# A graph layer's edge phase on TensorE as a loop, with its node phase and its loads reordered

## The chip, the core and the metric

The kernel runs on one core of a Trainium2 chip. A core has five engines that run their own instruction streams and meet only through semaphores: TensorE (PE, matrix products and transposes), VectorE (DVE), ScalarE (ACT), GpSimd (POOL) and SyncE (SP, which here only issues DMAs). The time is that of one execution on the device, in microseconds (us). The profile is of one execution of its own, whose time stands beside the others below.

## What is computed

The layer has 6250 nodes with 64 features and 200,000 directed edges, sorted by their destination. Each node is normed and goes through a small two-layer network. Each edge takes its two nodes' vectors, mixes them through three matrices and eight basis values, applies a second small network, and adds the outcome to its destination node.

```python
h = jnp.maximum(_layernorm(x, axis=-1), 0.0)
p1 = jnp.tanh(h @ pp_W1 + pp_b1) @ pp_W2 + pp_b2
inter = jnp.concatenate([p1[idx_i], p1[idx_j]], axis=-1)
inter = inter @ pi_W1 + pi_b1
inter = inter @ pi_W2 + pi_b2
inter = inter @ pi_W3
inter = inter.reshape(inter.shape[0], D, N_BASIS)
i1 = jnp.einsum('ecb,eb->ec', inter, basis)
i1 = jnp.tanh(i1 @ ii_W1 + ii_b1) @ ii_W2 + ii_b2
out = jax.ops.segment_sum(i1, idx_j, num_segments=p1.shape[0])
x = x + out
```

## The kernel before

**Node phase.** The matrices before the edge's basis values are linear, so the kernel folds them. A node's share as source (`u_tab`, 64 floats a row) and its share as destination (`v_tab`, three bf16 parts that sum to the float) are computed once for each node and stored to memory. For this PE transposes and multiplies the weights (L914, L918, L930; the products L925 to L928 make one constant that later becomes the bias `s_bias`), then takes the nodes in seven chunks: transposes (L873), first layer (L885), u rows (L891, copied by DVE at L610 and stored by SP at L298), and behind them v rows (stored at L306). The local places of each edge within its group, `loc_tab`, are stored too (L301).

**Edge phase.** The sorted edges are taken in 391 groups of 512 (`NG`), four tiles of 128. All engines run over the same steps. Step n does on PE, in this order: `sum_v(n)` (L982), which spreads the destination rows of a window of 42 nodes (`v_win`) over the edges by the one-hot `hot_t`; `place_rows(n)` (L987), which adds the gathered source rows `u_rows` and raises `s_ready`; `transpose_parts(n)` (L993) and `spread_basis(n-1)` (L1000) for the basis values; `z_group(n-2)` (L1008), 16 products whose outcome ACT puts through tanh (L517); the sum over destinations of group n-3 (L1050); and the transposes of group n-2 (L1015), which wait for that tanh. ACT also copies the sums to `st_sb` (L529, four times a group) and casts the basis (L539) and `t_sb` (L520). DVE multiplies by the basis (L693), makes the one-hots (L748, L794), splits the basis values of a whole piece into bf16 parts (L720 to L733), and adds the sums of a window to `acc_all` (L773), which it sets to zero at L756.

POOL issues four indirect gathers (L385) for each group into a ring of 16 slots (`UR`). It waits for `s_ready` of the group 16 before. SP fetches for each group the places (`loc_bc`, L327) and the window (`v_win`, L331), two rings of four slots, and every 15 groups (`PIECE`) a piece of `src`, `dst` and the basis values (L273, L274). If the graph isn't of the expected kind a slow path is taken; L1018 on PE is the jump past one of the two. PE's edge phase is written out: every step has its own instructions, and what it waits for are constants.

## Time and profile before

| | us |
|---|---|
| runs, median of three (lowest, highest) | 2676.39 (2671.01, 2684.13) |
| the profiled execution | 2664.88 |
| its span on the core | 2663.1 |
| L385 POOL, 1564 gathers, busy | 1515.0 |
| L693 DVE, 391 products, busy | 893.0 |
| L1008 PE, 6256 products, busy | 972.3 |
| L529 ACT, 1564 copies, busy | 734.3 |

A row of the timeline gives start, duration, engine, line and operation, and in brackets how long the engine sat idle before it and what ended that. "issue" is a wait that nothing in the profile shows; "remote" is a release from a queue that the profile can't name. PEld is the loading of weights into the array. SPq is the queue of an engine's own instructions, in which its DMAs are issued. A row of windows gives, for each stretch, its length, the busy time of each engine and its number of instructions, the granted TensorE clock as a share of 2.4 GHz, the busy share of 16 DMA engines and their rate. Between about 165 and 2566 us the groups run with gathers beside them; ahead of that stands the start, and behind it a few groups whose gathers are all done.

### The profile page before, as it was taken

Reading aid. Unit: us, or ns where it says so; the run is one execution under the profiler, and the core shown is the slowest. Engines: PE = TensorE matmul, PEld = TensorE weight load, DVE = VectorE, ACT = ScalarE, POOL = GpSimd, SP = SyncE. Lnnn points to the kernel's source line nnn. Section 1 sums busy time; section 2 is a strip of 40 time slices with the busy share of each in tenths; the row PEclk is TensorE's granted clock in tenths of the full one; section 3 lists DMA queues with packets and bytes.
Section 4 is the critical chain, followed back from the end, with each engine's and each line's share of the span. In section 5 each row is a group of like instructions: output and inputs, shape, how many; then the busy total and the mean of one; then the engine's idle time right before and its main releaser. Section 6 shows DMA issues by size and latency. Waiting matters only on the chain.

```text
span 2663.1 us, 55773 instructions
## 1 busy us (share of the span) xinstructions
PE 1994.9 (75%) x20333; PEld 1278.1 (48%) x20333; DVE 1261.5 (47%) x1823; ACT 1145.2 (43%) x2799; POOL 1521.3 (57%) x1581
## 2 busy tenths in 40 slices
PE   4147777878777777777877777778777778777788
PEld 3024454545454444444554454445444555444556
DVE  4224544545444444444454454454454444454455
ACT  4124444444444444444444444444444444444454
POOL 2755655656666555656565666566566565566530
PEclk9568888888988889888788888888888887888898
DMA  3212212222222221222221221222222122221111
GB/s 95 71 32 47 51 44 47 50 45 48 51 48 46 48 47 44 51 45 46 48 51 42 49 49 45 49 48 45 49 48 50 43 48 49 46 49 46 43 41 35
DMA packets 311481, 128.38 MB, mean 48 GB/s; under 512 B 233447, under 2 KB 283481, under 8 KB 311209
## 3 DMA queue, kind: packets, MB, share of 16 engines
q1 hardware_dynamic: 260033, 73.19, 13.6%
q0 software_dynamic: 50048, 51.35, 9.0%
q8 instruction: 165, 2.70, 0.4%
q14 instruction: 107, 0.88, 0.1%
q10 hardware_dynamic: 1128, 0.26, 0.1%
HBM read 118.67 MB, written 6.00 MB: 47 GB/s over the span
## 4 chain that ended last, share of the span: by engine, by line
PE 68%; issue 18%; another core or an unknown queue 7%; ACT 4%; DMA 1%; ACTq 0%; DVE 0%; SPq 0%; DVEq 0%
PE bank L1008 32%; PE bank L987 10%; PE bank L1050 8%; PE bank L1015 8%; PE spread_ps L1000 5%; PE bank L982 3%; ACT st_sb L529 3%; PE bank L993 1%; ACT tt_sb L517 1%; DMA v_tab<-acc_all 1%; DMA z_bias<-L_gnn_ii_b 0%; PE spread_ps L1083 0%; ACT t_sb L520 0%; ACT o_sb L438 0%
## 5 line engine op out<-in xcount | busy, mean ns | idle before, releaser
L385 POOL DMA_INDIRECT u_rows<-u_tab,src_e x1564 | 1515.0, 969 | 1044.0 <-PE bank L987 598.4
L693 DVE TENSOR_TENSOR o_sb<-st_sb,spread_ps 128x2048 f32<-128x2048 f32 x391 | 893.0, 2284 | 354.6 <-PE spread_ps L1000 182.2
L1008 PE MATMUL bank<-o_sb,g_sb 128*64 128x256 f32 x6256 | 972.3, 460 | 101.9 <-issue 92.7
L529 ACT ACTIVATE st_sb<-bank,s_bias 64x256 f32<-64x256 f32 x1564 | 734.3, 470 | 14.9
L1008 PEld LDWEIGHTS bank<-o_sb,g_sb 128*64 128x64 f32 x6256 | 529.2, 165 | 402.6 <-issue 284.0
L1015 PE MATMUL bank<-ident,tt_sb 128*128 128x128 f32 x782 | 183.6, 319 | 477.3 <-issue 356.1
L773 DVE TENSOR_TENSOR acc_all<-acc_all,bank 65x42 f32 x391 | 76.4, 195 | 977.4 <-remote 739.4
L517 ACT ACTIVATE tt_sb<-bank,z_bias 128x256 f32<-128x256 f32 x391 | 185.5, 474 | 724.3 <-remote 420.2
L520 ACT COPY t_sb<-bank 128x256 f32<-128x256 f32 x391 | 146.5, 375 | 515.3 <-PE bank L1015 406.4
L1015 PEld LDWEIGHTS bank<-ident,tt_sb 128*128 128x128 f32 x782 | 83.3, 149 | 521.8 <-issue 384.4
L987 PE MATMUL bank<-ident,u_rows 128*128 128x128 f32 x1564 | 320.8, 335 | 0.0
L1050 PEld LDWEIGHTS bank<-hot,t_sb 128*65 128x65 f32 x3128 | 224.7, 144 | 178.2 <-issue 177.4
L1050 PE MATMUL bank<-hot,t_sb 128*65 128x42 f32 x3128 | 272.4, 240 | 3.2 <-issue 2.7
L987 PEld LDWEIGHTS bank<-ident,u_rows 128*128 128x128 f32 x1564 | 236.4, 217 | 40.5 <-issue 9.7
L1000 PE MATMUL spread_ps<-bt_sb,spread 24*128 24x128 bf16 x6256 | 181.6, 241 | 14.2 <-issue 14.1
L539 ACT CAST bt_sb<-bank 128x128 bf16<-128x128 f32 x391 | 104.7, 268 | 198.4 <-remote 88.9
L982 PE MATMUL bank<-hot_t,v_win 126*64 126x128 bf16 x1564 | 125.3, 243 | 35.8 <-issue 35.7
L1000 PEld LDWEIGHTS spread_ps<-bt_sb,spread 24*128 24x128 bf16 x6256 | 103.6, 102 | 89.8 <-issue 89.7
L748 DVE TENSOR_SCALAR hot_t<-loc_bc,iota_p 126x512 bf16<-126x512 bf16 x391 | 142.3, 364 | 3.1 <-DMA loc_bc<-loc_tab 1.8
L794 DVE TENSOR_TENSOR hot<-loc_e,iota_f 128x168 f32<-128x168 f32 x391 | 126.2, 323 | 0.0
L982 PEld LDWEIGHTS bank<-hot_t,v_win 126*64 126x64 bf16 x1564 | 57.5, 112 | 109.8 <-issue 109.8
L993 PE MATMUL bank<-ident_b,b_parts 128*128 128x128 bf16 x391 | 94.9, 243 | 0.0
(110 smaller groups left out, 276.9 us busy)
## 6 DMA issues: line engine op xcount, KB each, us to landing
loc_bc<-loc_tab SPq DMA_DIRECT2D x391, 126.0 KB
u_rows<-u_tab,src_e POOLq DMA_INDIRECT x1564
v_win<-v_tab SPq DMA_DIRECT2D x391, 15.8 KB
basis<-edge_attr SPq DMA_DIRECT2D x26, 240.0 KB
v_tab<-acc_all SPq DMA_DIRECT2D x6, 375.0 KB
u_tab<-u_rows SPq DMA_DIRECT2D x6, 250.0 KB
out<-x_sb SPq DMA_DIRECT2D x2, 750.0 KB
x_sb<-x SPq DMA_DIRECT2D x3, 375.0 KB
```

The costliest lines, as they stand in the source:

```text
L385: pool.indirect_dma_start(out=u_rows[:, g % UR, j, :], out_offset=None, in_=u_tab[:, :], in_offset=bass.IndirectOffsetOnAxis(ap=src_e[:, g ...
L517: return nc.scalar.activation(tt_sb[:, r, :], z_ps, ACT.Tanh, bias=z_bias[:, 0:1])
L520: return nc.scalar.copy(t_sb[:, r, :, 0:D].rearrange("p (h q) c -> p q h c", h=2), t_ps.rearrange("p (q h c) -> p q h c", q=2, h=2))
L529: last = nc.scalar.activation(tiles[h * D:(h + 1) * D, j], s_ps[r][part].rearrange("p (q e) -> p q e", q=2), ACT.Identity, bias=s_bias[par ...
L693: return nc.vector.tensor_tensor(o_sb[:, r, :, :].rearrange("p c (j e) -> p j c e", j=TILES), st_sb[:, r, :].rearrange("p (j e) -> p j e", ...
L748: nc.vector.tensor_scalar(hot_t[:, g % 2, :], loc_bc[0:3 * W, g % VR, :], iota_p[0:3 * W, 0:1], None, ALU.is_equal).then_inc(hot_t_ready, 1)
L982: nc.tensor.matmul(s_ps[g % 2][TWICE[j], q * P:(q + 1) * P], v_win[:, g % VR, :], hot_t[:, g % 2, tile * P:(tile + 1) * P], start=(q == 0) ...
L987: last = nc.tensor.matmul(s_ps[r][:, q * P:(q + 1) * P], rows[:, 2 * q:2 * q + 2, :].rearrange("p j k -> p (j k)"), ident[:], start=alone ...
L1000: last = nc.tensor.matmul(spread_ps[:, j, c * P:(c + 1) * P], spread[q, 2 * c:2 * c + 2, :].rearrange("p b k -> p (b k)"), bt_sb[q, r, :], ...
L1008: last = nc.tensor.matmul(z_ps[h * D:(h + 1) * D, 0:2 * P], g_sb[:, c, :], o_sb[:, r, c, 2 * h * P:(2 * h + 2) * P], start=(c == 0), stop= ...
L1015: last = nc.tensor.transpose(t_ps[:, q * P:(q + 1) * P], tt_sb[:, r, q * P:(q + 1) * P], ident[:])
L1050: last = nc.tensor.matmul(seg_ps, t_sb[:, g % 2, j, :], hot[:, g % HR, j, :], start=(j == 0), stop=(j == TILES - 1))
```

## The change

Three things change together.

1. PE's steps 0 to 15 are written out, steps 16 to 383 are a loop of 23 passes over 16 steps, and steps 384 to 395 are written out again. In the loop, values that waits compare with, and the place in `b_parts`, are computed by register instructions. A piece now has 16 groups in place of 15, so that places in the rings are constants within the body.
2. In the node phase `wraw` and `p2` have a semaphore of their own, `w2_in`, and PE's first products wait for these three loads alone. The products of the weights stand in a row ahead of the first transposes. The constant's products and the copy to `s_bias` stand behind the u rows. ACT does the three weight copies ahead of its first root, and norms and tanhs in another order. The u rows are now staged in the basis buffer's far columns.
3. SP issues piece 1 behind the stores of u and v, in place of ahead of `loc_tab`'s store, and then waits for the u stores too. DVE sets the sums to zero behind the first group's splits and one-hots, and waits for this ahead of its first sum.

```diff
-    PIECE = 15
-    PIECES = FULL // PIECE
+    PIECE = 16
+    PIECES = -(-FULL // PIECE)
+    UN = UR
+    LOOP_END = NG // UN * UN
...
-        u_out = u_rows[0:NP].rearrange("p r j d -> p (r j) d")
+        u_out = basis[0:NP, 8 * PIECE * NBT:8 * PIECE * NBT + NPP * D].rearrange("p (i d) -> p i d", d=D)
...
-            load_piece(1)
             sp.wait_ge(loc_made, 1)
             sp.dma_start(loc_tab.rearrange("(b q) e -> q b e", b=RB),
...
+            load_piece(1)
             sp.wait_ge(base_read, 2)
...
             sp.wait_ge(loc_stored, 16)
+            sp.wait_ge(u_stored, 16 * NC)
...
             with dve.If(is_fast):
-                nc.vector.memset(acc, 0.0).then_inc(acc_zero, 1)
                 split_first(0)
...
                 pick_t(0)
-                dve.wait_ge(acc_zero, 1)
+                zero_sums()
                 for n in STEPS:
+                    if n == 4:
+                        dve.wait_ge(acc_zero, 1)
...
             pe.wait_ge(consts, 1)
-            pe.wait_ge(weights_in, 16 * N_WEIGHTS)
+            pe.wait_ge(w2_in, 48)
...
-            transposes(0)
             pe.wait_ge(wprep_act, 2)
             for half in TWICE:
-                const = bank[6][half, 0:1]
-                nc.tensor.matmul(const, a12[:, 0, :], b2col[:], start=True, stop=False)
...
             last.then_inc(wprep_pe, 1)
+            transposes(0)
             transposes(1)
...
+            pe.wait_ge(weights_in, 16 * N_WEIGHTS)
+            for half in TWICE:
+                const = bank[6][half, 0:1]
...
+            def step(n, u, first, last_pass):
+
+                def of(lag):
+                    return has_group(n, u, lag, first, last_pass)
+
+                def seen(lag, more=0):
+
+                    return n + (u - lag + 1 + more)
+
+                if of(0):
+                    pe.wait_ge(v_in[u % VR], n * (16 // VR) + 16 * (u // VR + 1))
+                    pe.wait_ge(hot_t_ready, seen(0))
...
             with pe.If(is_fast):
-                for n in STEPS:
...
+                for u in range(UN):
+                    step(0, u, True, False)
+                with pe.Fori(UN, LOOP_END, UN) as n:
+                    for u in range(UN):
+                        step(n, u, False, False)
+                for n in range(LOOP_END, NG + 5, UN):
+                    for u in range(UN):
+                        step(n, u, False, True)
```

PE's instructions at a step's boundary in the written-out edge phase, before:

```order
L1050 MATMUL bank<-hot,t_sb 65x42 x3
L1015 MATMUL bank<-ident,tt_sb 128x128 [waits tt_ready]
L1015 MATMUL bank<-ident,tt_sb 128x128
L982 MATMUL bank<-hot_t,v_win 64x128 [waits st_ready,hot_t_ready,v_in3]
L982 MATMUL bank<-hot_t,v_win 64x128 x3
L987 MATMUL bank<-ident,u_rows 128x128 [waits u_in3]
L987 MATMUL bank<-ident,u_rows 128x128
L993 MATMUL bank<-ident_b,b_parts 128x128
L1000 MATMUL spread_ps<-bt_sb,spread 128x128 [waits o_ready,bt_ready]
```

After, on PE where the loop begins (L1036 are the transposes, L1003 is `sum_v`, L1008 `place_rows`, L1021 `spread_basis`):

```order
L1036 MATMUL bank<-ident,tt_sb 128x128
L1085 UNCONDITIONAL_BRANCH
L1085 ISA
L1050 REGISTER_ALU [waits v_in0]
L1052 REGISTER_ALU [waits hot_t_ready]
L1003 MATMUL bank<-hot_t,v_win 64x128 [waits st_ready]
L1003 MATMUL bank<-hot_t,v_win 64x128 x3
L1054 REGISTER_ALU
L1008 MATMUL bank<-ident,u_rows 128x128 [waits u_in0]
L1008 MATMUL bank<-ident,u_rows 128x128
L1057 ISA
L1014 REGISTER_ALU [waits part3_]
```

The same operations stand in the same order; register instructions stand between them, and at the end of the body the loop's own pair, `L1085 REGISTER_ALU` and `L1085 COMPARE_AND_BRANCH`, follows the last transposes.

PE's start in the node phase, before, where L873 are the first transposes and L925 to L928 the constant's products:

```order
L914 MATMUL bank<-ident,wraw 64x64 [waits weights_in,consts]
L914 MATMUL bank<-ident,wraw 64x64 x2
L918 MATMUL bank<-p,wt 64x64 [waits wprep_act]
L918 MATMUL bank<-p,wt 64x64
L873 MATMUL spread_ps<-ident,o_sb 128x125 [waits normed_v]
L873 MATMUL spread_ps<-ident,o_sb 128x125 x3
L925 MATMUL bank<-b2col,a 64x1 [waits wprep_act]
L926 MATMUL bank<-b2col,a 64x1
L927 MATMUL bank<-pb1col,p 64x1
L928 MATMUL bank<-ones,b2row 64x1
L930 MATMUL bank<-a,wt 64x128
```

After (L925 is now the weights' transpose, L884 the nodes' transposes):

```order
L925 MATMUL bank<-ident,wraw 64x64 [waits w2_in,consts]
L925 MATMUL bank<-ident,wraw 64x64 x2
L929 MATMUL bank<-p,wt 64x64 [waits wprep_act]
L929 MATMUL bank<-p,wt 64x64
L934 MATMUL bank<-a,wt 64x128 [waits wprep_act]
L934 MATMUL bank<-a,wt 64x128
L884 MATMUL spread_ps<-ident,o_sb 128x125 [waits normed_v]
L884 MATMUL spread_ps<-ident,o_sb 128x125 x3
```

The first wait is for `w2_in` in place of `weights_in`, and the constant's products are gone from this place.

SP's queue from the u stores on, before:

```order
L298 DMA u_tab<-u_rows 125x512 [waits u_ready] x6
L298 DMA u_tab<-u_rows 125x128 [waits u_ready]
L273 DMA src_e<-src 128x15x4
L273 DMA dst_e<-dst 128x15x4
L274 DMA basis<-edge_attr 128x15x32
L301 DMA loc_tab<-loc_rows 98x4x512 [waits loc_made]
L306 DMA v_tab<-acc_all 125x1536 [waits v_ready] x6
L306 DMA v_tab<-acc_all 125x384 [waits v_ready]
L310 TENSOR_LOAD fast [waits flag_ready,base_read]
L310 ISA x2
L315 COMPARE_AND_BRANCH [waits v_stored3,v_stored2,loc_stored,v_stored1,v_stored0]
```

After, where the same pieces load at L275 and L276:

```order
L300 DMA u_tab<-basis 125x512 [waits u_ready] x6
L300 DMA u_tab<-basis 125x128 [waits u_ready]
L302 DMA loc_tab<-loc_rows 98x4x512 [waits loc_made]
L307 DMA v_tab<-acc_all 125x1536 [waits v_ready] x6
L307 DMA v_tab<-acc_all 125x384 [waits v_ready]
L275 DMA src_e<-src 128x16x4
L275 DMA dst_e<-dst 128x16x4
L276 DMA basis<-edge_attr 128x16x32
L312 TENSOR_LOAD fast [waits flag_ready,base_read]
L312 ISA x2
L318 COMPARE_AND_BRANCH [waits v_stored3,loc_stored,v_stored2,u_stored,v_stored1,v_stored0]
```

Piece 1 moved behind the seven stores of v, and stands next to piece 2, which follows the jump.

## Rows read from the trace of the kernel before

**Rows 1.** Windows by stage, the columns in the first row.

```profile
core 0: us, PE busy (x) PEld busy (x) DVE busy (x) ACT busy (x) POOL busy (x), PEclk, DMA share, GB/s
90.00:165.00 75.00, 12.83 (x76) 6.57 (x77) 6.29 (x11) 6.80 (x16) 49.95 (x53) 0.50 0.16 37
165.00:1000.00 835.00, 643.95 (x6588) 411.09 (x6588) 402.99 (x563) 367.36 (x904) 498.27 (x516) 0.86 0.24 47
1000.00:2560.00 1560.00, 1216.99 (x12337) 773.07 (x12336) 752.36 (x1047) 689.58 (x1693) 934.53 (x968) 0.86 0.23 47
2562.00:2640.00 78.00, 75.58 (x906) 49.28 (x902) 53.41 (x75) 49.55 (x120) 3.54 (x4) 1.00 0.11 26
```

**Rows 2.** Windows of L385 alone: us, POOL busy (x), PEclk, DMA share, GB/s.

```profile
200.00:2560.00 2360.00, 1411.96 (x1464) 0.86 0.23 47
```

**Rows 3.** Waits of POOL, 200 to 2560 us: total, times, longest.

```profile
POOL u_rows L385 <- PE bank L987: 580.2, 338, 4.8
```

**Rows 4.** Timeline, 1003 to 1018 us: start, duration, instruction [idle before <-releaser].

```profile
1007.28 1.07 POOL L385 DMA_INDIRECT u_rows<-u_tab,src_e  x1 [1.68 <-PE bank L987]
...
1007.33 1.95 PE L1008 MATMUL bank<-o_sb,g_sb 128*64 128x256 f32 x16
...
1010.82 0.47 ACT L517 ACTIVATE tt_sb<-bank,z_bias 128x256 f32<-128x256 f32 x1 [1.64 <-remote]
1011.16 0.94 POOL L385 DMA_INDIRECT u_rows<-u_tab,src_e  x1 [0.30 <-issue]
...
1011.35 0.44 PE L1015 MATMUL bank<-ident,tt_sb 128*128 128x128 f32 x2 [1.47 <-issue]
```

**Rows 5.** Timeline, ACT alone, 2595 to 2625 us.

```profile
2598.83 0.47 ACT L517 ACTIVATE tt_sb<-bank,z_bias 128x256 f32<-128x256 f32 x1
...
2602.98 0.47 ACT L517 ACTIVATE tt_sb<-bank,z_bias 128x256 f32<-128x256 f32 x1
...
2607.14 0.47 ACT L517 ACTIVATE tt_sb<-bank,z_bias 128x256 f32<-128x256 f32 x1
```

**Rows 6.** The page: DMA queue of the instructions.

```profile
q8 instruction: 165, 2.70, 0.4%
```

**Rows 7.** L1018 (the jump past the slow path): ns least/median/most.

```profile
L1018 PEldq COMPARE_BRANCH  x2: 78/205/332, 74.9 to 2640.5; - x2
```

**Rows 8.** Timeline, 80 to 104 us.

```profile
83.96 6.82 POOL L385 DMA_INDIRECT u_rows<-u_tab,src_e  x1 [0.30 <-issue]
...
84.10 5.61 DVE L756 MEMSET acc_all<- 65x6656 f32 x1 [11.06 <-issue]
...
91.34 0.35 SPq L327 DMA_DIRECT2D loc_bc<-loc_tab  x1
...
94.25 0.40 DVE L748 TENSOR_SCALAR hot_t<-loc_bc,iota_p 126x512 bf16<-126x512 bf16 x1 [1.79 <-DMA loc_bc<-loc_tab]
```

**Rows 9.** Waits, 20 to 56 us.

```profile
POOL u_rows L385 <- DMA u_tab<-u_rows: 47.1, 1, 47.1
PE bank L914 <- DMA z_bias<-L_gnn_ii_b: 21.6, 1, 21.6
```

**Rows 10.** Timeline, 14 to 60 us.

```profile
25.28 0.37 PE L925 MATMUL bank<-b2col,a 64*64 64x1 f32 x2 [1.10 <-ACT a L460]
...
27.03 0.37 PE L928 MATMUL bank<-ones,b2row 1*64 1x1 f32 x2
...
36.04 10.44 SPq L298 DMA_DIRECT2D u_tab<-u_rows  x7
...
48.10 5.24 SPq L273 DMA_DIRECT2D dst_e<-dst  x1
```

**Rows 11.** Windows, 44 to 48 us, columns as in group 1.

```profile
44.00:48.00 4.00, 3.75 (x40) 3.52 (x39) 2.48 (x7) 2.67 (x4) 0.00 (x0) 1.00 0.31 105
```

**Rows 12.** Timeline, POOL alone, 96 to 170 us.

```profile
154.86 0.95 POOL L385 DMA_INDIRECT u_rows<-u_tab,src_e  x1 [0.30 <-issue]
```

**Rows 13.** Waits, 90 to 165 us.

```profile
DVE o_sb L693 <- remote: 51.8, 1, 51.8
```

More of the change, by code:

```diff
@@ L313, in _ @@
             sp.wait_ge(loc_stored, 16)
+            sp.wait_ge(u_stored, 16 * NC)
             with sp.If(is_fast):
[L316 to L332 removed]
+                for n in range(NG):
+                    if has(n):
+                        g = n
+                        k = g // PIECE + 2
+                        if g % PIECE == 0 and k < PIECES:
+                            if k >= LD:
+                                sp.wait_ge(part1, k - LD + 1)
+                            load_piece(k)
+                        if g == (PIECES - 2) * PIECE:
+                            load_last()
+                        start = sp.value_load(base_row[0:1, g:g + 1], min_val=0, max_val=N - W)
+                        if g >= VR:
+                            sp.wait_ge(hot_t_ready, g - VR + 1)
+                        sp.dma_start(loc_bc[0:3 * W, g % VR, :], loc_tab[g:g + 1, :].to_broadcast(
+                            [3 * W, GE])).then_inc(loc_in[g % VR], 16)
+                        if g >= VR:
+                            sp.wait_ge(s_ready, g - VR + 1)
+                        sp.dma_start(v_win[:, g % VR, :], v_tab[bass.ds(start, W), :, :].rearrange("n w d -> w n d")
+                                     ).then_inc(v_in[g % VR], 16)
             with sp.Else():
@@ L470, in _ @@
             relu(2)
+            norm(5, 1)
             tanh(1)
-            norm(5, 1)
+            relu(3)
             norm(6, 1)
-            for c in range(3, NC):
+            tanh(2)
+            for c in range(4, NC):
                 relu(c)
@@ L749, in pick_t, with zero_sums @@
                                         ALU.is_equal).then_inc(hot_t_ready, 1)
-            dve.wait_ge(v_ready, NC)
-            for i in range(VPR):
-                dve.wait_ge(v_stored[i], V_STORES[i])
+            def zero_sums():
+                dve.wait_ge(v_ready, NC)
+                for i in range(VPR):
+                    dve.wait_ge(v_stored[i], V_STORES[i])
+                nc.vector.memset(acc, 0.0).then_inc(acc_zero, 1)
             with dve.If(is_fast):
-                nc.vector.memset(acc, 0.0).then_inc(acc_zero, 1)
                 split_first(0)
@@ L976, in _, with has_group, ring, sum_v @@
             is_fast = pe.value_load(fast[0:1, 0:1], min_val=0, max_val=1)
-            def sum_v(g):
+            def has_group(n, u, lag, first, last_pass):
+                if first:
+                    return u >= lag
+                return not last_pass or n + u - lag < NG
+            def ring(n, size, u):
+                return slice(n % size + u, n % size + u + 1) if isinstance(n, int) else bass.ds((n + u) & (size - 1), 1)
+            def sum_v(u):
                 for q in range(2):
@@ new lines, in step @@
+            def step(n, u, first, last_pass):
[6 more added lines that the diff above has]
+                    pe.wait_ge(hot_t_ready, seen(0))
+                    if of(2):
+                        pe.wait_ge(st_ready, seen(2))
+                    sum_v(u)
+                    pe.wait_ge(u_in[u], n * (64 // UR) + 64)
+                    place_rows(u_rows[:, u, :, :], u % 2, False).then_inc(s_ready, 1)
+                    if u == 0:
+                        pe.wait_ge(part3, (n >> 4) + 1)
+                    transpose_parts(b_parts[:, ring(n, 2 * PIECE, u), :, :], u % 2).then_inc(bt_ps_ready, 1)
+                if of(1):
+                    pe.wait_ge(bt_ready, seen(1))
+                    if of(2):
+                        pe.wait_ge(o_ready, seen(2))
+                    spread_basis((u - 1) % 2).then_inc(spread_ready, 1)
+                if of(2):
+                    pe.wait_ge(o_ready, seen(2))
+                    if of(3):
+                        pe.wait_ge(t_ready, seen(3))
+                    z_group(u % 2).then_inc(z_ready, 1)
+                if of(3):
+                    pe.wait_ge(t_ready, seen(3))
+                    pe.wait_ge(hot_ready, seen(3))
+                    if of(4):
+                        pe.wait_ge(acc_done, seen(4))
+                    for j in range(TILES):
+                        last = nc.tensor.matmul(seg_ps, t_sb[:, (u - 3) % 2, j, :], hot[:, (u - 3) % HR, j, :],
+                                                start=(j == 0), stop=(j == TILES - 1))
+                    last.then_inc(seg_ready, 1)
+                if of(2):
+                    pe.wait_ge(tt_ready, seen(2))
+                    t_transposes(u % 2).then_inc(t_ps_ready, 1)
```

107 lines of the change are left out of this document (27 added, 80 removed).

## The prediction, made before the changed kernel ran

> **What bounds the kernel now.** I read the windows by stage first. From 165 to 2560 us, nine tenths of the span, PE is busy 77 to 78% of the time at a granted clock of 0.86 and no engine is full [rows 1]. The reader should see there that the last stage, 2562 to 2640 us, does the same groups with POOL silent: PE busy 75.58 of 78 us and clock 1.00. The timeline of ACT gives the period there, tanh starting at 2598.83, 2602.98 and 2607.14 us, so 4.15 us per group [rows 5]. Before that a group takes 2360 us / (1464 gathers / 4) = 6.45 us [rows 2]. The difference, 2.3 us per group, is there only while POOL gathers.
>
> POOL is not simply full: it is busy 1411.96 of 2360 us [rows 2] and waits 580.2 us in 338 waits, 1.7 us each, for PE's place_rows at L987 [rows 3]. One step shows how the two hold each other [rows 4]. POOL's four gathers run from 1007.28 to 1012.10 us, a burst of 4.8 us. PE's z_group (L1008) is over at 1009.28, yet ACT's tanh, which waits for it, starts at 1010.82, and PE's transposes L1015 wait 1.47 us for that. Then PE runs sum_v and place_rows of the next step, which free POOL's slot, and POOL waits again. So the period is one burst plus a PE stretch behind it: 4.8 + 1.7 = 6.5 us. Time added to PE between tanh and place_rows lengthens this chain one for one; time taken from PE's queue elsewhere gives nothing.
>
> **Part 1, the loop.** Before, PE's instructions for the edge phase are one straight row of some 40,000; after, 16 steps are one loop body passed 23 times, with 22 jumps back, and 28 steps are written out around it.
>
> *Fetching less code.* The queue of instructions moved 165 packets, 2.70 MB, 0.4% of 16 engines' span [rows 6]: 0.004 x 16 x 2663 / 165 = 1.03 us per packet of 16 KB, one for 246 of the 40,666 loads and matmuls, 0.4 per group. All of it is at most 170 us of one DMA engine out of sixteen, fetched ahead of use, and DMA engines are busy only 23% [rows 1]. I cost its disappearance at 0. What hides it is that the next block comes while this one runs; the loop's end is where that cover is gone.
>
> *The jump back.* The body is 16 steps of about 110 instructions, some 1750, seven such blocks that touch eight. The trace has no backward jump. It has a forward one, L1018, 78 to 332 ns [rows 7]; its target lies near. Lower end, if the target is held: 0.1 to 0.3 us x 22 = 2 to 7 us. If the target's block must be fetched, PE stands still for one small transfer. The packet alone is 1.03 us; the nearest whole chain is loc_bc: issued at 91.34, its user on DVE starts at 94.25, 2.9 us [rows 8]. The last instructions ahead of the jump are the two transposes L1015, 0.44 us [rows 4], which cover so much of it and no more, since the sequencer stands at their wait for tanh and cannot run ahead. So one miss costs 1.03 - 0.44 = 0.6 us at least and 2.9 us at most; if the second block isn't ready either, 4.2. I take the value nearest to the whole chain without the 0.35 us of its issue: 2.9 - 0.35 - 0.44 = 2.1 us, times 22 = **+46 us** (13 to 92). It falls on the path: behind the jump stand sum_v and place_rows, for which POOL waits. What is late next is POOL's burst, then everything.
>
> The Trainium skill ("Runtime: NRT & Kernel Launch", Instruction fetch mechanics) says that a taken branch whose target isn't in the current two-page window forces a fetch before execution goes on. No row of this case shows a backward jump; by that rule the term is the miss just costed. The same section gives PE a store of 2048 instructions; by that figure a body of 1750 would stay in it and the term would be the lower end, a total near 2676 us.
>
> *Register instructions.* The waits' values are now computed: by the order of the instructions some 3.5 register instructions more per group, at L1050, L1014 and the like. Least time of a sequencer instruction in the rows is 78 ns [rows 7], so 0.27 us per group. They cost that only where the array waits for the sequencer. Behind the wait for tanh [rows 4] the computed values are those of v_in and hot_t_ready and the address at L1014; the array has loads and matmuls of 0.7 us queued around the latter. I take 0; if all of it is exposed, 0.27 x 368 = 100 us.
>
> **Part 2, the node phase.** PE's first products no longer wait for z_bias, the last of eleven weights, which came at 21.6 us [rows 9]. Eight products for the constant move off the path to the u rows: from 25.28 to 27.40 us, 2.1 us [rows 10]. What the start gives goes through POOL: it waited 47.1 us for the u stores [rows 9] and started at about 54.5. The stores are issued from 36.04 [rows 10] and are 1.56 MB; at 105 GB/s [rows 11] they are 15 us, but took 18.5, since piece 1's columns go between them at 48.10 [rows 10] and the last stores wait. Moving piece 1 gives 3.4 us back, the products 2.1, together 5.5. One more table load on ACT (its root before the tanh) lies under the PE products.
>
> **Part 3, pieces behind the stores, the memset behind the first group.** While piece 2 was loaded one gather took 6.82 us, 5.9 more than the others [rows 8]. Now pieces 1 and 2 follow one another there, both under POOL's filling: 0 to 5.9 us more. I take 1.5. The memset of 5.61 us [rows 8] leaves the front of the first group, where it hid behind the v stores, and stands ahead of the fourth; DVE has 51.8 us of waiting there [rows 13], so 0 either way.
>
> How much of this arrives at the end? DVE stands from 112 to 164 us [rows 13], and the others behind it, until POOL's ring is full: 16 slots and three freed, 76 gathers, the last at 154.86 [rows 12]; from 54.5 us that is 76 x 1.25 + 5.9 = 101. The end of this stretch moves with POOL's start alone, however early PE and DVE are: -5.5 + 1.5 = **-4 us** (-15 to +1).
>
> **Sum.** 2664.9 (the profiled execution, span 2663.1) + 46 - 4 + 0 = 2707. That execution is 11.5 us under the median of 2676.4, so I add the same +42 to the median: **2718 us**.
>
> **Rivals.**
>
> *The loop stays held, or its first block does* (chance 0.27). 22 jumps at 0.1 to 0.3 us are 2 to 7, against -4: 2674 to 2679 us, no change. For it speaks that the one jump in the trace costs 0.33 at most [rows 7]. Against it, that in the trace the instructions come one block at a time, 246 loads and matmuls per packet (40,666 / 165), just ahead of use: nothing shows that old blocks are kept. By the store of 2048 instructions in the Trainium skill ("Runtime: NRT & Kernel Launch", Instruction fetch mechanics) it would come out so; by the two-page window of the same section it would not.
>
> *Faster* (0.17). The jump is cheap and the start gives more: POOL's filling begins up to 9 us earlier because PE's early products also let the whole chain of node chunks move up, and the long gather appears once, not twice. It decides from about -13 us in all. Also here is the case that code fetching does disturb PE in the 6.45 us groups: 0.4 fetches per group at 0.1 to 0.2 us are 15 to 30 us. 2640 to 2662 us; taken 2658. Against it: groups in which a packet arrives are no longer than the others by more than their share.
>
> *Slower through the register instructions* (0.11). The sequencer isn't ahead of the array at sum_v, since it stood at the wait for tanh. Then 0.1 to 0.27 us for 368 groups are 37 to 100 us, with or without the jumps: 2710 to 2765, taken 2740. The mark is a longer period in every group, in place of one long group in sixteen.
>
> *The jumps cost, as forecast* (0.45): 2718 us, between 2690 and 2765.
>
> **How the numbers follow.** Slower by over 0.5% (13 us, about what a measurement of this kernel can tell from no change; three runs of before lie 13 us apart) is the forecast and the register case, 0.45 + 0.11 = 0.56. Same is the held loop, 0.27. Faster is 0.17. The range goes from the upper half of the faster case, 2655, to two missed blocks at each jump, 2765, and leaves out about 0.15.
>
> **What would show it.** Right: every sixteenth group has a gap on PE of 2 to 3 us between the transposes and sum_v, 22 of them, and POOL's wait ahead of it is longer by as much; packets of the instruction queue stay near 165 or rise to about 8 x 23. If the packets fall to some 25, the loop is held and the forecast is wrong. If the last stage, without gathers, has a period over 4.15 us only inside the loop, the register instructions cost. POOL's first gather should start near 49 us and the first long stand of DVE end near 160. Wrong altogether would be a period in the middle that differs from 6.45 us by 0.1 or more in all groups: then the interplay of POOL's bursts and PE, on which I count as unchanged, has moved.

## The result and the profile after

The changed kernel took 2784.0 us in the median of four runs (2778.76 to 2795.19), before 2675.8 us in four runs: 1.0416 times before, 95% interval 1.0383 to 1.0448, so slower by 108 us. The profiled execution took 2778.8 us, its span was 2776.9 us.

The page's busy times and queues, which answer to the windows [rows 1] and to the queue of instructions [rows 6]:

```profile
PE 2024.7 (73%) x20333; PEld 1290.0 (46%) x20333; DVE 1258.8 (45%) x1813; ACT 1146.1 (41%) x2800; POOL 1512.1 (54%) x1581
...
PEclk8579888887898888888878888898788888888898
...
q8 instruction: 218, 3.57, 0.5%
```

No engine has more work than before: PE has the same 20,333 products, which took 1994.9 us there. The queue of the instructions, which brings PE's code in packets of 16 KB, moved 218 packets in place of 165. The windows by stage:

```profile
core 0: us, PE busy (x) PEld busy (x) DVE busy (x) ACT busy (x) POOL busy (x), PEclk, DMA share, GB/s
...
1000.00:2560.00 1560.00, 1179.32 (x11730) 744.31 (x11724) 711.53 (x988) 654.03 (x1608) 885.53 (x920) 0.83 0.23 45
...
2640.00:2740.00 100.00, 89.69 (x1051) 58.24 (x1049) 61.56 (x88) 58.15 (x143) 23.07 (x24) 0.95 0.15 35
```

Between 1000 and 2560 us PE did 11,730 products in place of 12,337 [rows 1], at a clock of 0.83 for 0.86. POOL's waits for PE, with L1008 now the line of `place_rows`, against the 580.2 us of [rows 3] (the stretch here is 200 to 2660 us, 100 us longer, as the kernel is):

```profile
POOL u_rows L390 <- PE bank L1008: 718.9, 353, 8.1
```
```profile
PE bank L1003 <- issue: 77.7, 22, 3.8
...
PE spread_ps L1021 <- issue: 23.4, 31, 1.2
```

The row to see is L1003, `sum_v`: 77.7 us in 22 waits, up to 3.8 us, ended by nothing but PE's own issuing. Before, it had none. 22 is the number of jumps. The loop's jump (least/median/most in ns):

```profile
L1085 PEldq COMPARE_BRANCH  x23: 79/3481/3822, 343.2 to 2717.8; - x23
```

The last of the 23 branches isn't taken and took 79 ns. The 22 taken ones took 3.5 us. This is one of them, at 452.3 us, in the timeline of all engines; a quiet step stands in [rows 4]:

```profile
451.65 0.47 ACT L524 ACTIVATE tt_sb<-bank,z_bias 128x256 f32<-128x256 f32 x1 [2.27 <-PE bank L1029]
...
452.17 0.44 PE L1036 MATMUL bank<-ident,tt_sb 128*128 128x128 f32 x2 [0.44 <-issue]
...
456.29 0.42 PE L1003 MATMUL bank<-hot_t,v_win 126*64 126x128 bf16 x4 [3.68 <-issue]
...
456.64 1.22 PE L1008 MATMUL bank<-ident,u_rows 128*128 128x128 f32 x4
...
457.65 0.31 PE L1014 MATMUL bank<-ident_b,b_parts 128*128 128x128 bf16 x1
...
457.90 0.39 PE L1021 MATMUL spread_ps<-bt_sb,spread 24*128 24x128 bf16 x5
458.00 0.27 ACT L546 CAST bt_sb<-bank 128x128 bf16<-128x128 f32 x1 [4.48 <-PE bank L1014]
...
458.61 0.94 POOL L390 DMA_INDIRECT u_rows<-u_tab,src_e  x1 [6.56 <-PE bank L1008]
...
458.94 0.50 PE L1021 MATMUL spread_ps<-bt_sb,spread 24*128 24x128 bf16 x11 [0.65 <-issue]
...
459.37 3.68 PE L1029 MATMUL bank<-o_sb,g_sb 128*64 128x256 f32 x16
459.58 2.29 DVE L700 TENSOR_TENSOR o_sb<-st_sb,spread_ps 128x2048 f32<-128x2048 f32 x1 [5.60 <-PE spread_ps L1021]
...
463.10 0.47 ACT L524 ACTIVATE tt_sb<-bank,z_bias 128x256 f32<-128x256 f32 x1 [3.02 <-issue]
```

PE ends the transposes L1036 at 452.61 and begins `sum_v` at 456.29: it stood 3.68 us. Inside `spread_basis` it stood once more, 0.65 us, after 5 of 16 products. Behind that z_group took 3.68 us for what takes 1.95 at full clock [rows 4]; from 459.4 to 463.0 us the granted clock was 0.50, the lower of its two levels. ACT's tanh of this step starts 11.45 us after the one before, against some 6.4. POOL waited 6.56 us. The granted clock in the 11 us of the stand (0.83 over the stage):

```profile
452.00:463.00 11.00, 6.50 (x44) 3.45 (x44) 2.99 (x4) 2.53 (x7) 3.53 (x5) 0.62 0.13 29
```

Of 16 places in the loop's body the one with the jump had a mean of 11.45 us from tanh to tanh, and 6.30 at the same place before: 5.2 us in each pass. The other 15 together came to 97.5 us and 96.5 before.

### The profile page after: what moved, and what is told of

It reads as the page before. It is cut to its first block, busy times and chain, and to the rows that moved or that the text cites. A ratio compares the mean times of both kernels' runs of the same rounds, so it can differ in the third digit from the quotient of the medians.

```text
span 2776.9 us, 57046 instructions
## 1 busy us (share of the span) xinstructions
PE 2024.7 (73%) x20333; PEld 1290.0 (46%) x20333; DVE 1258.8 (45%) x1813; ACT 1146.1 (41%) x2800; POOL 1512.1 (54%) x1581
## 4 chain that ended last, share of the span: by engine, by line
PE 63%; issue 18%; another core or an unknown queue 12%; ACT 4%; DVE 1%; DVEq 0%; ACTq 0%; DMA 0%
PE bank L1029 29%; PE bank L1008 10%; PE bank L1075 7%; PE bank L1036 6%; PE spread_ps L1021 6%; PE bank L1003 3%; ACT st_sb L536 3%; PE bank L1014 1%; ACT tt_sb L524 1%; DVE hot_t L754 0%; DMA v_tab<-acc_all 0%; DVE o_sb L700 0%; PE spread_ps L1117 0%; DVEq L778 0%
## 5 line engine op out<-in xcount | busy, mean ns | idle before, releaser
L1036 PE MATMUL bank<-ident,tt_sb 128*128 128x128 f32 x782 | 182.9, 318 | 458.5 <-issue 361.3
L1008 PE MATMUL bank<-ident,u_rows 128*128 128x128 f32 x1564 | 329.4, 342 | 0.0
L1036 PEld LDWEIGHTS bank<-ident,tt_sb 128*128 128x128 f32 x782 | 83.5, 149 | 502.4 <-issue 393.4
L1008 PEld LDWEIGHTS bank<-ident,u_rows 128*128 128x128 f32 x1564 | 243.4, 223 | 42.0 <-issue 12.9
L1021 PE MATMUL spread_ps<-bt_sb,spread 24*128 24x128 bf16 x6256 | 193.2, 244 | 59.5 <-DVE o_sb L700 35.5
L1003 PE MATMUL bank<-hot_t,v_win 126*64 126x128 bf16 x1564 | 127.8, 247 | 137.1 <-issue 130.9
L1021 PEld LDWEIGHTS spread_ps<-bt_sb,spread 24*128 24x128 bf16 x6256 | 106.7, 102 | 140.4 <-issue 140.1
L1003 PEld LDWEIGHTS bank<-hot_t,v_win 126*64 126x64 bf16 x1564 | 58.9, 114 | 212.7 <-issue 204.4
```

Source lines behind the costliest of these rows:

```text
L1003: nc.tensor.matmul(s_ps[u % 2][TWICE[j], q * P:(q + 1) * P], v_win[:, u % VR, :], hot_t[:, u % 2, tile * P:(tile + 1) * P], start=(q == 0) ...
L1008: last = nc.tensor.matmul(s_ps[r][:, q * P:(q + 1) * P], rows[:, 2 * q:2 * q + 2, :].rearrange("p j k -> p (j k)"), ident[:], start=alone ...
L1021: last = nc.tensor.matmul(spread_ps[:, j, c * P:(c + 1) * P], spread[q, 2 * c:2 * c + 2, :].rearrange("p b k -> p (b k)"), bt_sb[q, r, :], ...
L1036: last = nc.tensor.transpose(t_ps[:, q * P:(q + 1) * P], tt_sb[:, r, q * P:(q + 1) * P], ident[:])
```

## The experiments

Some words first. A packet of PE's code holds 256 instructions: in the trace of e6_quarter_written, where PE runs straight on, there are 256.06 recorded instructions of PE for each packet. Such a stretch of code is called a block here, and the place of an instruction is its position within its block, 0 to 255. A jump back misses when its target's code is no longer held by PE and has to be fetched again. The head is the loop's first instruction.

Two kinds of chip have to be told apart, since the runs fell on several. In the first measurement (whose chip isn't on record) and on two chips later before took 2670 to 2760 us ("slow kind" in the expectations), on three others 2074 to 2075 us ("quick kind"). Every ratio is to runs of before on the same chip. `e5` to `e8`, `e10` and `e11` are read across chips. That can be done because their ordinary groups all take 4.15 to 4.17 us, on either kind.

| run | PE's edge phase | before | this | ratio (95%) |
|---|---|---|---|---|
| first result | loop, 22 jumps | 2675.8 | 2784.0 | 1.0416 (1.0383 to 1.0448) |
| after_again | the same | 2670.1 | 2778.1 | 1.0418 (1.0373 to 1.0462) |
| after_third | the same | 2758.0 | 2867.3 | 1.0393 (1.0363 to 1.0424) |
| e9_again | head at a block's start | 2758.0 | 2766.1 | 1.0026 (1.0002 to 1.0051) |
| e9_aligned | head at a block's start | 2074.2 | 2065.6 | 0.9958 (0.9941 to 0.9974) |
| e1_written | written out | 2074.9 | 2067.0 | 0.9960 (0.9946 to 0.9975) |
| e1_again | written out | 2073.9 | 2064.7 | 0.9957 (0.9942 to 0.9971) |
| e2_hint | jump announced | 2074.9 | 2065.4 | 0.9955 (0.9939 to 0.9972) |
| e2_again | jump announced | 2073.9 | 2065.7 | 0.9958 (0.9942 to 0.9975) |
| e3_body64 | 64 steps, 4 jumps | 2074.9 | 2067.6 | 0.9965 (0.9949 to 0.9982) |
| e4_rotated | jump behind z_group | 2074.9 | 2068.6 | 0.9964 (0.9950 to 0.9978) |

With one gather per group, single runs:

| run | PE's edge phase | us | packets of code |
|---|---|---|---|
| e6_quarter_written | written out | 1750.1 | 165 |
| e5_quarter_loop | loop as changed | 1933.1 | 218 |
| e8_quarter_rotated | jump behind z_group | 1861.4 | 218 |
| e7_quarter_aligned | head at place 0 | 1754.8 | 20 |
| e10_quarter_slot32 | head at place 32 | 1751.4 | 20 |
| e11_quarter_slot56 | head at place 56 | 1795.8 | 65 |

### Written out, announced, longer, moved

The theory was that the jumps wait for their code and nothing else of the change costs. The main rival was a cost of the register instructions in every group.

`e1_written`:

```diff
-                with pe.Fori(UN, LOOP_END, UN) as n:
+                for n in range(UN, LOOP_END, UN):
```

> The changed kernel with PE's steps 16 to 383 written out again instead of looped; everything else of the change stays. Theory (the jump back misses its code: 23 branches of 3.48 us median in the changed kernel's trace, one group of 11.45 us per pass in place of 6.3): the whole loss goes, and the start's gain stays, which is 8.0 us at the first tanh and 11.7 us at group 16. So 2676 - 8 to 12 = 2664 to 2668 us. Rival (the loss is in the new piece size, the moved loads or the moved zeroing, not in the loop): stays near 2784 us.

`e2_hint`:

```diff
-                with pe.Fori(UN, LOOP_END, UN) as n:
+                with nc.Fori(UN, LOOP_END, UN, engines=[mybir.EngineType.PE], hint_back_edge=True) as n:
```

`e3_body64`:

```diff
+    BODY = 4 * UN
...
-                with pe.Fori(UN, LOOP_END, UN) as n:
+                with pe.Fori(UN, UN + 5 * BODY, BODY) as n:
+                    for u in range(BODY):
+                        step(n, u, False, False)
+                for n in range(UN + 5 * BODY, LOOP_END, UN):
                     for u in range(UN):
                         step(n, u, False, False)
```

> The changed kernel with 64 steps in the loop body and 5 passes, so 4 jumps in place of 22; 320 of the 391 groups still run in the loop with register instructions in every one. Theory (a price per jump of 5.3 us, the change's 2784 less 2666 by 22): 2666 + 4 x 5.3 = 2687 us. Rival (a price per looped group, 118 us / 368 = 0.32 us): 2666 + 320 x 0.32 = 2768 us.

`e4_rotated`, where `close` is the rest of a step from the segment sums on:

```diff
                 with pe.Fori(UN, LOOP_END, UN) as n:
                     for u in range(UN):
+                        close(n, u - 1, False, False)
                         step(n, u, False, False)
...
```

> The changed kernel with the loop cut at another place of the step: the jump stands right behind the 16 products of z_group, ahead of the segment sums and the transposes, still 22 jumps. At this place the array has 1.95 us of products queued, and behind them PE waits for ACT's tanh, some 1.4 us more. Theory (a fixed sequencer stall of 3.5 us that costs only what isn't covered): 0 to 1 us shows per jump instead of 5.3, so 2666 to 2690 us, with the branch itself still at 3.5 us. Rival (each pass costs what it costs wherever the jump stands, by fetching or by registers): stays near 2784 us.

These four fell on a chip where before took 2075 us, and all came out at 2065 to 2069 us. The times therefore tell nothing of what the jump costs on the first chip, and the changed kernel itself was never timed on such a chip. What they tell is where a jump can hide. The page of e1_written there, and a step in its timeline:

```profile
POOL 1777777777777777777777777777777777777772
...
POOL 66%; issue 22%; PE 8%; DMA 1%; DVE 1%; SPq 1%; ACTq 1%; ACT 0%; DVEq 0%; POOLq 0%
```
```profile
1005.23 1.95 PE L1029 MATMUL bank<-o_sb,g_sb 128*64 128x256 f32 x16
...
1007.22 0.47 ACT L524 ACTIVATE tt_sb<-bank,z_bias 128x256 f32<-128x256 f32 x1
...
1009.22 0.71 PE L1008 MATMUL bank<-ident,u_rows 128*128 128x128 f32 x4 [0.79 <-DMA u_rows<-u_tab,src_e]
```
```profile
POOL u_rows L390 <- issue: 434.3, 1425, 0.3
...
PE bank L1008 <- DMA u_rows<-u_tab,src_e: 203.8, 151, 2.4
```

POOL issues one gather after another at 1.25 us, with almost no waiting for PE (0.9 us in all from 200 to 2000 us), 5.0 us per group, and is the bound. ACT's tanh starts at 1007.22, right at the end of z_group at 1007.18, where it lagged 1.5 us in [rows 4]. Before 1009.22 PE waits 0.8 us for gathered rows, 203.8 us in all, and a ring of 16 groups stands between them. So a stand of 3.5 us every 80 us can be made up. e4_rotated shows that: its branches took 3.6 us in the mean, PE stood 22 times for 42.1 us before L1084, the segment sums with which the moved body begins, and in return waited 155.4 us for gathered rows against 209.7 in e2_hint; the time differs by 3 us.

```profile
PE bank L1008 <- DMA u_rows<-u_tab,src_e: 155.4, 120, 2.7
PE bank L1084 <- issue: 42.1, 22, 2.5
```

```profile
L1085 PEldq COMPARE_BRANCH  x23: 80/216/267, 223.1 to 1997.4; - x23
```
```profile
q8 instruction: 20, 0.33, 0.1%
```

The body is then fetched once and stays: 13 packets come up to 209.4 us, and the next at 2001.6, behind the loop.

### One gather per group: PE as the bound on any chip

To price the jump where PE is the bound, POOL was given one gather of four. These kernels leave out three quarters of the source rows, so they don't compute the layer; they serve for the timing alone.

```diff
+            nc.gpsimd.memset(u_rows[:, :, 1:, :], 0.0)
...
-                    for j in range(TILES):
+                    for j in range(1):
                         pool.indirect_dma_start(
...
-                    pe.wait_ge(u_in[u], n * (64 // UR) + 64)
+                    pe.wait_ge(u_in[u], n * (16 // UR) + 16)
```

> The twin: one gather per group in place of four, the other rows zero, with PE's steps written out. 391 x 4.15 + some 110 us of start and 25 us of end = 1758 us if POOL's gathers are what separates 4.15 from 5.0 or 6.45 us; the looped one is longer by the jumps.

> The changed kernel with one gather per group in place of four; the other three quarters of the gathered rows are zeros, set once. So POOL needs 1.25 us per group and PE sets the pace everywhere, as in the last stage of before, 4.15 us per group. With its twin that has PE written out it gives the price of a jump where PE is the bound: 3.5 - 0.4 = 3.1 us by the branch alone, so 22 x 3.1 = 68 us more than the twin; if the lower clock behind the stall costs too, up to 5 us each, 110 us more. If the price of 5.3 us on the slow chip is made by POOL's bursts alone, 68 us here.

The written-out twin came at 1750 us for an expected 1758: the gathers are what separates 4.16 from 6.45 us per group. The loop took 183 us more, 8.3 us for each of 22 jumps, above every theory. The mean period of the place with the jump was 12.05 us, the next 4.69, and the 14 others 4.15 to 4.17, as in the twin. So the register instructions cost 0.00 us here, and all of it is at the jump:

```profile
299.36 0.44 PE L1037 MATMUL bank<-ident,tt_sb 128*128 128x128 f32 x2
...
303.94 0.30 PE L1004 MATMUL bank<-hot_t,v_win 126*64 126x128 bf16 x4 [4.14 <-issue]
...
305.23 0.39 PE L1022 MATMUL spread_ps<-bt_sb,spread 24*128 24x128 bf16 x5
...
307.13 0.50 PE L1022 MATMUL spread_ps<-bt_sb,spread 24*128 24x128 bf16 x11 [1.51 <-issue]
...
307.57 3.68 PE L1030 MATMUL bank<-o_sb,g_sb 128*64 128x256 f32 x16
...
311.30 0.47 ACT L525 ACTIVATE tt_sb<-bank,z_bias 128x256 f32<-128x256 f32 x1 [3.89 <-PE bank L1030]
```
```profile
290.00:300.00 10.00, 9.75 (x116) 6.19 (x112) 7.42 (x9) 6.91 (x18) 1.93 (x2) 1.00 0.24 46
300.00:311.00 11.00, 5.55 (x41) 2.98 (x41) 3.38 (x5) 2.25 (x6) 0.95 (x1) 0.70 0.11 27
311.00:321.00 10.00, 10.00 (x120) 6.62 (x119) 5.96 (x10) 6.63 (x16) 1.89 (x2) 0.99 0.14 32
```
```profile
307.60:311.20 3.60, 3.60 (x20) 1.70 (x17) 2.29 (x1) 0.00 (x0) 0.00 (x0) 0.50 0.17 45
```

Three parts can be read: 4.14 us of standing before `sum_v`; 1.51 us amid `spread_basis`, where the next block begins (its packet starts at 304.3 us, takes 1.36, and PE goes on 1.5 us after that); and a PE at half its clock until about 311 us, whose z_group takes 3.68 us for 1.95. The windows show the granted clock fall from 1.00 to 0.70 in the 11 us around the stand, and stand at 0.50 under z_group. 4.14 + 1.51 is 5.7. The other 2.7 of the 8.3 is the remainder, which the slower array accounts for: z_group alone is 1.7 of it.

> The looped kernel with one gather per group (other gathered rows zero), and the jump behind z_group's 16 products in place of behind the transposes. Here PE is the bound. Theory (what is queued for the array covers the sequencer's stand): 1.95 us of products cover it in place of 0.44, so 1.5 us less for each jump, and less low clock behind it: 8.3 - 1.5 to 8.3 - 3, 1867 to 1900 us. Rival (the place of the jump is of no account): 1933 us.

1861.4 us, 72 us less for the same 22 misses, 3.3 each: the rival fell, and the theory's span of 1867 to 1900 was passed at its good end. PE stood 2.1 us at a time there in place of 4:

```profile
PE bank L1085 <- issue: 46.5, 22, 2.4
PE spread_ps L1022 <- issue: 6.8, 13, 1.0
```

### Where the loop's first instruction lies

```diff
-                with pe.Fori(UN, LOOP_END, UN) as n:
+                with nc.Fori(UN, LOOP_END, UN, engines=[mybir.EngineType.PE],
+                             head_slot={mybir.EngineType.PE: 0}) as n:
```

> The looped kernel with one gather per group (other gathered rows zero, as in e5), and the loop's first instruction placed at the start of a block of code. In e5 a jump cost 8.3 us: 4.1 the branch, 1.5 a second stand of PE amid spread_basis, where the next block begins 97 instructions behind the head, and the rest the lower clock behind it. Theory: with a whole block behind the head the second stand goes and the branch stays; 1.5 us less or a little more for the clock, so 22 x 1.5 = 33 us under e5's 1933 us: 1900 us. Rival (the second stand is not the next block): stays at 1933 us.

1754.8 us: both expectations were far off. Not the second stand alone but every miss went. The branches, beside a queue of 20 packets:

```profile
L1086 PEldq COMPARE_BRANCH  x24: 76/208/328, 157.9 to 1694.0; - x24
```

In this trace no packet of PE's code comes between 219 us and 1696 us. The group with the held jump takes 4.45 us for 4.16, so a held jump costs 0.3 us. The second stand tells where the blocks lie in e5 and in the changed kernel: counted from the head, PE stands after 14 products with their 14 loads and 8 instructions of its own, so the next block of 256 begins 36 instructions behind the head. (The expectation's 97 was a wrong count.) The head is then at place 220, and the body of 1752 ends at 1972, 180 into its eighth block. With the head at 0 it takes seven. (The body's 1752 instructions can be counted in the trace of e7, from one branch to the next.) So two positions were tried, `head_slot` 32 (the body ends at 1784 of 1792) and 56 (at 1808):

> One gather per group, loop head at place 32 of its block. The body has about 1752 instructions, so it ends at 1784, within seven blocks of 256 (1792). Theory (the store holds eight blocks, the body and the next one fetched ahead of use must fit): as with head 0, 20 packets, branches 0.2 us, 1755 us. Rival (the head must be at a block's start for the jump to hit): 1900 to 1935 us, over 200 packets.

> One gather per group, loop head at place 56 of its block, so the body ends at 1808 and touches eight blocks. Theory (eight blocks and one fetched ahead don't fit in eight): every jump misses, 218 packets or a few less, branches of 3.5 to 4 us; 200 instructions stand behind the head in its block, so the second stand is shorter than in e5 or gone; 1755 + 22 x (6.8 to 8.3) = 1905 to 1935 us. Rival (what matters is room behind the head, or nearness to the block's start): 1755 us.

Place 32 behaved as place 0, 1751.4 us and 20 packets: it isn't the block's start that matters. Place 56 went wrong in a way that I hadn't expected: 65 packets, and one branch in four slow, at 4.8 to 5.9 us.

```profile
L1086 PEldq COMPARE_BRANCH  x24: 76/216/5870, 159.2 to 1734.9; - x24
```
```profile
PE bank L1004 <- issue: 31.7, 21, 6.0
```

Five such jumps for 44.4 us more than place 32 are 8.9 us each. 65 less 20 is 5 times 9 packets. The changed kernel's 218 packets are made the same way: 14 up to the first jump, 9 on each of the 22 passes that a jump begins, and 6 behind the loop, in e5, e4_rotated and e8 too. The body touches eight blocks, so the ninth packet is the block behind the body, fetched ahead and never run until the loop ends. A body that reaches 16 instructions into an eighth block loses its code on every fourth pass; one that reaches 180 into it, as in the changed kernel, on every pass; one within seven never. That fits a store of eight blocks with the next one fetched ahead into it, which drives out the head when the body itself fills eight. The store's size and order are inferred from these counts; nothing in a trace shows them directly. The announced loop fits too: if its head lies where e5's does, its body touches eight blocks, and its 13 packets ahead of the first jump are one fewer than in the changed kernel, so the ninth block isn't fetched. The Trainium skill ("Runtime: NRT & Kernel Launch", Instruction fetch mechanics) gives PE's store as 2048 instructions, eight blocks of 256, and these runs agree; its "only 2 cache lines" doesn't fit them. Why place 56 misses every fourth time is not explained by a trace.

### With all gathers, on both kinds of chip

> The changed kernel with the loop's first instruction at the start of a block of 256 instructions, all gathers in place. With one gather per group this made the branches 0.2 us and the queue's packets 20. Theory (misses make the whole loss): ratio 0.996 to before on a chip of the slow kind, as on one of the quick kind. Rival (register instructions, piece size or moved loads cost when POOL's bursts and PE hold each other): over 1.005 on the slow kind.

> The written-out version again, for its profile and one time on a chip of the slow kind. Theory: 8 to 12 us under before and equal to the aligned loop within 6 us. Rival as with the aligned loop: register instructions cost, then this one is faster than the aligned loop by 20 us or more.

> The kernel with PE's steps written out and all else of the change, once more, since its first measurement was on a chip of the quick kind (before 2075 us), where no wait of PE is on the path. On a chip of the slow kind (before about 2670 us). Theory (the jumps make the whole loss): 8 to 12 us under before, ratio 0.996. Rival (piece size, moved loads or zeroing cost on the slow kind): ratio over 1.0, up to 1.04.

> The looped kernel with the announcement of its jump at the loop's head, once more, for a chip of the slow kind. On the quick chip its branches took 0.22 us and the instruction queue moved 20 packets in place of 218. Theory: 22 jumps of 0.2 us under cover and no fetching are nothing, ratio 0.996 as for the written-out one. Rival (fetching of code disturbs PE or POOL): faster than the written-out kernel by 0.2 us for each of the 145 packets it saves, 29 us, ratio 0.985. Rival (register instructions cost while POOL gathers): ratio 1.01 or more.

All four fell on chips where before takes 2074 us, where POOL is the bound and none of their rivals on the slow kind could show. They repeat 0.996 for written out, announced and aligned alike (e1_third: 2062.8 us in one run). The changed kernel was then run against the kernel before twice more, and the last time together with the aligned loop.

> The changed kernel as it is, on the chip of this call. On the chip of the first measurement it was 1.042 of before. On the chip of the runs that followed, before took 2075 us in place of 2676, and its gathers set the pace. Theory (the jump costs 3.5 us of PE each time, and shows only where PE is on the path): on a chip of the quick kind the ring of 16 gathered groups bridges it, ratio 0.995 to 1.000, waits for gathered rows shrink by as much; on a chip of the slow kind 1.04 again. Rival (the jump reaches the end everywhere): 22 x 3.3 = 73 us, ratio 1.03 on the quick kind too.

> The kernel before as it is, for a profile on the chip of this call. If it is of the quick kind: POOL's gathers in one row without waits for PE, 4 x 1.25 = 5.0 us per group, ACT's tanh right behind PE's products. If of the slow kind: 6.45 us per group again, with tanh 1.5 us behind the products while POOL gathers.

> The changed kernel as it is. Theory: on a chip of the quick kind (before near 2075 us) POOL's gathers set the pace, PE's stand of 3.5 us at each jump is made up out of its slack of 0.8 us per group, and the ratio is 0.996 to 1.000; on one of the slow kind (before near 2670) 1.042 as twice before. Rival: 22 stands of 3.3 us reach the end on the quick kind too, ratio 1.03.

> The changed kernel with the loop's first instruction at a block's start, so that its jumps take 0.2 us. Theory (misses make the whole loss): on a chip of the slow kind 0.994 to 0.997, some 110 to 120 us under the changed kernel; on the quick kind 0.996. Rival on the slow kind (register instructions, piece size or moved loads cost a share): over 1.005.

Both times the chip was one where before takes 2670 us or more. before_again, 2681.5 us, showed 6.50 us per group as before. The changed kernel repeated its loss. The aligned loop lost 101.2 of the 109.3 us, 4.6 us per jump. The misses are the loss, then; but 1.0026 isn't the expected 0.994 to 0.997, and this is the one place where the rival keeps a share.

```profile
PE bank L1036 <- ACT tt_sb L524: 168.4, 74, 4.7
...
PE bank L1003 <- issue: 3.2, 14, 0.3
```
```profile
q8 instruction: 20, 0.33, 0.0%
```

The stands are gone (L1003 3.2 us, 20 packets), the first tanh comes at 156.4 us as in the changed kernel (below), 8 us ahead of the first measurement's kernel before, and yet the end is 8 us behind before. There is no trace of the kernel before on this chip, so the 8 us of the start is taken over from another, and the interval (1.0002 to 1.0051) leaves 1 to 14 us for the end. What takes some 16 us over 375 groups there, 0.04 us each, wasn't found: register instructions between PE and POOL's bursts, pieces of 16, or the phase that the groups settle into. PE waits more for ACT's tanh (168.4 us, where after_third has 124.9 and before_again 127.6). The written-out version would tell, and it never met such a chip.

## Why the prediction was wrong

**The bound.** That PE and POOL hold each other, and that a stand of PE between tanh and place_rows reaches the end, was right, for the chip of the profile. On other chips the program is bound by POOL alone (e1_written). That the period elsewhere stays unchanged held nearly: 6.50 us at the other 15 places, 6.43 before.

**The jump.** The mechanism and the count were right: 22 misses, the gap between the transposes and sum_v, long groups one in sixteen, and packets near 165 or up to 8 x 23 = 184 (it was 218, of which 22 x 9 = 198 belong to the passes behind a miss: one block more than the eight that I had, and 22 times, not 23). The term was mis-sized: 2.1 us for each, +46 in all, and 4.6 measured (e9_again against after_third), +101, more than even my upper end of 4.2 and +92. The step that failed is the price of a miss, in three ways. The branch takes 3.5 us, more than the 2.9 us of the nearest whole chain [rows 8], which I had even shortened by its issue: in the rows of the changed kernel a packet starts 0.9 to 1.2 us behind the branch's start, takes 0.9 to 1.5, and the branch ends 1.3 to 1.5 us after that. A second block is missed, which I had only as the upper bound. And a PE that has stood comes back at the lower clock; I had no term for that, though [rows 1] shows a clock of 0.50 where PE stands a lot. 2784.0 lay above the range of 2655 to 2765. Of the 66 us between 2718 and 2784, this term is 55 (101 for 46). The start gave 4 us more than forecast, and the other 15 match the 16 us that e9_again leaves unexplained, a cost that I had at 0.

**What I left out** in the count of the body: I wrote "seven such blocks that touch eight" and went on. That one clause held the whole case: whether the body takes seven blocks or eight decides whether its jump misses. The rival of the held loop (2674 to 2679) was nearly right for the same body with its head elsewhere in the block (e9_again, 1.0026 of before).

**Fetching less code**, costed at 0: right. Where PE is the bound, e6_quarter_written took 1750.1 us with 165 packets and e10_quarter_slot32 1751.4 with 20, and in e6 groups in which a packet starts took 4.16 us like the others. The remark under *Faster*, that such groups are no longer in the kernel before, doesn't hold as it stands: in its trace they took 6.60 us in the mean, the others 6.34, with a spread of 0.95 from group to group. But e9_again fetches nothing in its loop and isn't faster than before.

**Register instructions**, costed at 0: right where PE is the bound: 4.16 us in loop and twin, and also in the changed kernel itself, whose last eight periods inside the loop, behind the last gather, are 4.15 to 4.16 us, the sign that I had named. With POOL's bursts up to 0.04 us per group stay possible, against the 0.27 us that I had as the most.

**The start**, -4 us: it gave -8.0, the first tanh at 156.4 in place of 164.4 us. POOL's first gather came at 48.6 us where I had said 49. The reasoning between the two failed. No gather was lengthened: the longest now takes 1.42 us, where [rows 8] has 6.82. But POOL stood once for 11.43 us, ahead of the gather at 149.96, for a queue that the profile can't name. So the 76th gather started at 153.70 us, only 1.2 ahead of the 154.86 of [rows 12], though the first was 5.9 ahead; and the first tanh was 8.0 ahead all the same. The end of this stretch does not move with POOL's start alone. What it waits for wasn't followed up.

```profile
149.96 0.94 POOL L390 DMA_INDIRECT u_rows<-u_tab,src_e  x1 [11.43 <-remote]
...
153.70 0.94 POOL L390 DMA_INDIRECT u_rows<-u_tab,src_e  x1 [0.30 <-issue]
```
```profile
L390 POOL DMA_INDIRECT u_rows<-u_tab,src_e x1564: 938/944/1419, 48.6 to 2680.0; - x196
```

**The moved zeroing**, 0: nothing contradicts it.

## What to carry to other kernels

Before a written-out stream is turned into a loop, count the body in blocks of 256 instructions from where its head will lie: here 1752 instructions in seven blocks never missed, and in eight they missed on every pass, which cost 101 us on one chip (on every fourth pass, where the body reached only 16 instructions into the eighth). Moving the head removed this. Announcing the jump kept the code held too, but was timed only where POOL is the bound. Place the jump where the array has work queued and where what waits for PE has slack. Measure on more than one chip: the change was 1.042 on one, and a version with all 22 misses, its jump behind z_group (e4_rotated), was 0.996 on another.

## What the runs showed of the hardware

- A taken branch to code that isn't held took 3.5 us in the mean (4.0 in e5), to held code 0.21 us, and 0.08 when not taken.
- A body of seven blocks stayed with PE: in e7 14 packets and then none for 1476 us. A body that touches eight was fetched anew, with a ninth block, on each of 22 passes. With an announcement of the jump (BRANCH_PREFETCH_HINT, 31 ns each pass) it stayed held.
- In e5, after a stand of 4.1 us, the granted clock was low for about 7 us (0.54 from 303.9 to 311.2 us, 0.99 from 311.2 to 315), z_group taking 3.68 us for 1.95.
- Chips come in two kinds for this kernel: before took 2074 to 2075 us on three chips, and 2670 to 2758 in three measurements, on two chips or three. The gathers are as fast on both, but on the second kind, while POOL gathers, ACT's tanh starts 1.5 us (median of the kernel before, 300 to 2500 us) after the products that it waits for, against 0.05 us on the first kind. On the second kind it is 0.05 us too once the gathers are over, and in e5 with a quarter of them. On the slowest chip (before 2758 us) the median was 1.64 us in after_third. Why is open.
